# A cross-attention and mixture-of-experts layer: another order in the prologue, and the last token tile in a PSUM bank of its own

## The reference

```python
x = x + attention(_layernorm(x), ctx, ctx, mask)       # q = LN(x) Wq + bq, k = ctx Wk + bk, v = ctx Wv + bv
xf = _layernorm(x).reshape(-1, 256)
scores = sigmoid(_l2norm(xf) @ _l2norm(gate_w).T)      # (4096, 16)
topk_scores, topk_idx = top_k(scores, 8)
combine = one_hot(topk_idx) * topk_scores / sum(topk_scores)
routed = sum_e combine[:, e] * (silu(xf @ w_gate[e]) * (xf @ w_up[e])) @ w_down[e]
shared = silu(xf @ sw_gate) * (xf @ sw_up) @ sw_down
x = x + routed + shared
```

## Time and profile before

| | |
|---|---|
| median of 3 runs | 641.28 us (640.98 to 641.42) |
| profiled execution | 641.74 us, of which span 639.6 us |
| TensorE busy | 99% of the span |
| VectorE, ScalarE, GpSimd busy | 73%, 37%, 43% |
| TensorE in the chain that ended last | 92% |

### The profile page before, as it was taken

One profiled execution on the slowest core, in us unless ns is written; L12 is line 12 of the kernel. 1 busy time (PEld: TensorE's weight loads), 2 busy tenths in 40 slices (PEclk: granted clock), 3 DMA queues, 4 the chain that ended last, 5 costly groups with the idle time before them and its releaser, 6 DMA issues.

```text
span 639.6 us, 10415 instructions
## 1 busy us (share of the span) xinstructions
PE 632.1 (99%) x3690; PEld 550.9 (86%) x3690; DVE 464.7 (73%) x925; ACT 234.6 (37%) x500; POOL 275.4 (43%) x261
## 2 busy tenths in 40 slices
PE   8999999999999999999999999999999999999997
PEld 7688888988889888888888888888888888888886
DVE  3789887759876698767977689766987669575444
ACT  4745544332343324333242333324233332432221
POOL 2527576325533356233653346423562335423342
PEclk9999999999999999999999999999999999999999
DMA  7457562532315324333335232253151431242100
GB/s 206 100 178 218 162 169 44 201 101 73 83 35 182 109 67 99 111 107 119 68 68 188 70 117 66 34 200 108 67 98 38 162 109 46 53 133 101 66 2 33
DMA packets 112512, 67.04 MB, mean 105 GB/s; under 512 B 80981, under 2 KB 102254, under 8 KB 112462
## 3 DMA queue, kind: packets, MB, share of 16 engines
q1 hardware_dynamic: 111374, 65.61, 35.4%
q10 hardware_dynamic: 1088, 0.79, 0.4%
HBM read 55.66 MB, written 10.42 MB: 103 GB/s over the span
## 4 chain that ended last, share of the span: by engine, by line
PE 92%; DVE 3%; DMA 1%; issue 1%; ACT 1%; POOL 1%; SPq 1%; POOLq 0%; ACTq 0%; DVEq 0%
PE gate_ps L399 9%; PE gate_ps L398 9%; PE y_ps L397 9%; PE up_ps L399 9%; PE up_ps L398 9%; PE gate_ps L397 9%; PE y_ps L398 9%; PE up_ps L397 9%; PE y_ps L399 9%; PE f_ps L545 3%; PE up_ps L406 1%; PE f_ps L582 1%; SPq L277 1%; PE f_ps L584 1%; DMA xs<-t_rows 1%
## 5 line engine op out<-in xcount | busy, mean ns | idle before, releaser
L1358 POOL TENSOR_TENSOR hidden<-hidden,cb 128x512 f32<-128x512 f32 x128 | 193.3, 1511 | 288.6 <-DVE hidden L1162 245.6
L880 ACT ACTIVATE hidden<-gate_ps 128x512 f32<-128x512 f32 x136 | 81.3, 598 | 295.0 <-PE gate_ps L399 294.9
L1158 DVE SCALAR_TENSOR_TENSOR hidden<-hidden,gate_ps 128x512 f32<-128x512 f32 x136 | 92.7, 682 | 97.5 <-ACT hidden L880 97.2
L397 PE MATMUL y_ps<-W,hs 128*128 128x256 f32 x544 | 154.2, 283 | 0.6 <-DVE hs L1168 0.6
L398 PE MATMUL y_ps<-W,hs 128*128 128x256 f32 x544 | 151.5, 278 | 0.0
L399 PE MATMUL y_ps<-W,hs 128*128 128x256 f32 x544 | 151.2, 278 | 0.0
L1168 DVE TENSOR_TENSOR hs<-hidden,hs 128x512 fp32r<-128x512 f32 x136 | 105.6, 777 | 22.6 <-ACT hs L887 22.2
L397 PEld LDWEIGHTS y_ps<-W,hs 128*128 128x128 f32 x544 | 102.2, 188 | 7.4 <-issue 1.6
L397 PE MATMUL gate_ps<-xT,W 128*128 128x512 f32 x272 | 107.3, 394 | 0.0
L399 PE MATMUL gate_ps<-xT,W 128*128 128x512 f32 x272 | 107.1, 394 | 0.0
L399 PE MATMUL up_ps<-xT,W 128*128 128x512 f32 x272 | 106.9, 393 | 0.0
(11 more groups left out here) (164 smaller groups left out, 641.1 us busy)
## 6 DMA issues: line engine op xcount, KB each, us to landing
cb<-c_rows SPq DMA_DIRECT2D x64, 512.0 KB, 4.5
blocks<-in_x_dram SPq DMA_DIRECT2D x28, 128.0 KB, 2.9
xin<-in_x_dram SPq DMA_DIRECT2D x7, 512.0 KB, 3.7
t_rows<-blocks SPq DMA_DIRECT2D x28, 128.0 KB, 2.7
xs<-t_rows SPq DMA_DIRECT2D x7, 512.0 KB, 3.6
out_dram<-x SPq DMA_DIRECT2D x7, 512.0 KB, 5.8
p_rows<-blocks SPq DMA_DIRECT2D x28, 80.0 KB, 2.3
stage<-in_L_ffn_w_gate_dram SPq DMA_DIRECT2D x16, 128.0 KB, 2.7
```

What stands on the lines that cost most here:

```text
L397: mm(ps, lh, rh, start=first and i == 0, stop=False)
L880: af(ew[:, i, :], gate_ps[:, i, :], ACT.Tanh, scale=0.5).then_inc(tanh_done, 1)
L1158: V_.scalar_tensor_tensor(out=ew[:, i, :], in0=ew[:, i, :], scalar=1.0, in1=gate_ps[:, i, :], op0=ALU.add, op1=ALU.mult).then_inc(silu_don ...
L1358: pg.tensor_tensor(h[:, i, :], ew[:, i, :], cb[:, pair % PLACES, (e - 1) % 2, :], ALU.mult) \
```

## The change

Three parts. (1) *Prologue.* Wq's load is issued ahead of Wk's and its turns stand first on PE, before ctx; `write_wqT` moves from ACT to DVE, behind `mean_wq` and ahead of `ln1(0, 0)`; the warm-up has 17 turns; SP issues the ctx tails ahead of x and both halves of x ahead of the small vectors; `load_x_blocks(1)` moves ahead of stage 4's load. (2) *Attention ahead.* PE does the scores ahead of the other batches' turns, both turns of the probabilities around `values(0)`, and `attend` ahead of `keys_rest(1)`; `turn_ln2_first` ahead of `keys_by_wq_rest(0)`; `keys_by_wq_rest(1)` behind `turn_z(0)`. ACT's list follows: `split_hi(0)` ahead of the first `exps`, `split_hi(1)` behind `read_keys_rest(1)`. POOL's list is not changed. (3) *Tail.* In the last chunk tile 3 of y is accumulated in `f_ps[:, 0]`; tiles 2 and 3 are added and stored one by one.

```diff
-WARM = 20
+WARM = 17
+        def y_of(c, j):
+            if c == CHUNKS - 1 and j == TILES - 1:
+                return f_ps[:, 0, 0:D]
+            return y_ps[:, j // 2, (j % 2) * D:(j % 2 + 1) * D]
...
             def store_last():
-                for q in range(2):
-                    sp.wait_ge(y_added, upto(CHUNKS - 1, 2, q + 1 + FREE))
-                    sp.dma_start(out_rows[CHUNKS - 1, :, 2 * q:2 * q + 2, :], x2[:, 1, 2 * q:2 * q + 2, :]) \
-                        .then_inc(stored, 16)
+                for i, (j0, j1) in enumerate(((0, 2), (2, 3), (3, 4))):
+                    sp.wait_ge(y_added, upto(CHUNKS - 1, 2, i + 1 + FREE))
+                    sp.dma_start(out_rows[CHUNKS - 1, :, j0:j1, :], x2[:, 1, j0:j1, :]).then_inc(stored, 16)
...
             sp.dma_start(ctx_main[:, 0, :], ctx[0, 0:P, :]).then_inc(ctx0_loaded, 16)
-            sp.dma_start(xin[:, 0:2, :], x_rows[0][:, 0:2, :]).then_inc(x_half, 16)
             sp.wait_ge(tail_zeroed, 1)
             for b in range(B):
                 sp.dma_start(ctx_tail[PAD * b:PAD * b + TAIL, :], ctx[b, P:KEYS, :]).then_inc(ctx0_loaded, 16)
+            sp.dma_start(xin[:, 0:2, :], x_rows[0][:, 0:2, :]).then_inc(x_half, 16)
+            sp.dma_start(xin[:, 2:4, :], x_rows[0][:, 2:4, :]).then_inc(x_loaded, 16)
...
-            sp.dma_start(xin[:, 2:4, :], x_rows[0][:, 2:4, :]).then_inc(x_loaded, 16)
...
             load_stage(STAGES)
+            load_x_blocks(1)
             load_stage(STAGES + 1)
-            load_x_blocks(1)
             move_v_tails()
@@ tensor
             def keys_by_wq_first():
                 pe.wait_ge(wqT_read, 1)
+                pe.wait_ge(kt_read, 2)
...
+                    alone = c == CHUNKS - 1 and j >= 2
-                    ins = three_pass(y_ps[:, j // 2, (j % 2) * D:(j % 2 + 1) * D],
+                    ins = three_pass(y_of(c, j),
...
+                                     first=e == 0 and (j % 2 == 0 or alone),
+                                     last=e == NE - 1 and (j % 2 == 1 or alone))
+                    if e == NE - 1 and (j == 1 or c == CHUNKS - 1 and j == 2):
                         ins.then_inc(y_half, 1)
...
             keep_warm()
+            turn_wq()
             turn_ctx_first()
             turn_x_first(0)
             keys_first()
-            turn_wq()
-            bias_row_first()
             turn_x_first(1)
             keys_by_wq_first()
+            bias_row_first()
+            scores(0, 0)
+            scores(0, 1)
             turn_ctx_rest(0)
             turn_ctx_rest(1)
-            scores(0, 0)
-            scores(0, 1)
             value_tails()
+            turn_p_first(0)
             values(0, y_ps[:, 0, 0:D])
-            turn_p_first(0)
+            turn_p_first(1)
             keys_rest(0)
-            turn_p_first(1)
-            keys_rest(1)
             attend(0, 0)
             attend(0, 1)
+            keys_rest(1)
             values(1, y_ps[:, 0, 0:D])
             turn_router()
             bias_row_rest()
-            keys_by_wq_rest(0)
             turn_ln2_first(0)
             turn_ln2_first(1)
-            keys_by_wq_rest(1)
+            keys_by_wq_rest(0)
             logits(0)
             gate(0, 0)
             turn_z(0)
+            keys_by_wq_rest(1)
             up(0, 0)
@@ scalar
+                act.dma_start(wq_in, Wq.rearrange("(k p) e -> p k e", p=P)).then_inc(wq_loaded, 16)
                 act.dma_start(wk_in, Wk.rearrange("(k p) e -> p k e", p=P)).then_inc(wk_loaded, 16)
-                act.dma_start(wq_in, Wq.rearrange("(k p) e -> p k e", p=P)).then_inc(wq_loaded, 16)
...
             write_keep(0, 2)
-            write_wqT()
+            read_t1_first(1)
+            read_a_first()
+            bias_row_first()
+            write_keep(2, 4)
             read_ctx_tails()
-            bias_row_first()
             router_norms()
-            read_a_first()
-            read_t1_first(1)
-            write_keep(2, 4)
+            split_hi(0)
+            exps(0, 0)
             read_ctx_rest(0)
             read_ctx_rest(1)
-            split_hi(0)
-            split_hi(1)
-            exps(0, 0)
             exps(0, 1)
...
             read_keys_rest(1)
+            split_hi(1)
             split_hi(2)
@@ vector
+            def write_wqT():
+                dve.wait_ge(wq_mean, 1)
+                for m in range(KD):
+                    ins = V_.tensor_scalar(wqT[:, m, :], gate_ps[:, 0, m * D:(m + 1) * D], wq_sum[:, KD + m:KD + m + 1],
+                                           None, ALU.add)
+                ins.then_inc(wqT_read, 1)
...
+            def add_y_last():
+                c = CHUNKS - 1
+                for i, (j0, j1) in enumerate(((0, 2), (2, 3), (3, 4))):
+                    if i < 2:
+                        dve.wait_ge(y_half, CHUNKS + i)
+                    else:
+                        dve.wait_ge(down_done, upto(c, NE, NE + FREE))
+                    v = x2[:, c % 2, j0:j1, :].rearrange("p j d -> p (j d)")
+                    V_.tensor_tensor(v, v, y_ps[:, 0, :] if i == 0 else y_of(c, j0), ALU.add).then_inc(y_added, 1)
...
             dve.sem_inc(y_added, FREE)
+            mean_wq()
+            write_wqT()
             ln1(0, 0)
             spread_bq()
-            mean_wq()
             ln1(0, 1)
```

More of the change, by code:

```diff
@@ L385, in _ @@
             store_last()
-            sp.wait_ge(stored, 16 * (CHUNKS + 1 + FREE))
+            sp.wait_ge(stored, 16 * (CHUNKS + 2 + FREE))
         @block.tensor
@@ L633, in down @@
                     t = slice(j * P, (j + 1) * P)
-                    ins = three_pass(y_ps[:, j // 2, (j % 2) * D:(j % 2 + 1) * D],
+                    alone = c == CHUNKS - 1 and j >= 2
+                    ins = three_pass(y_of(c, j),
                                      [((hs[:, i, HI, t], hs[:, i, LO, t]),
                                        (W[:, e, HI, DN0:DN0 + D], W[:, e, LO, DN0:DN0 + D]))],
-                                     first=e == 0 and j % 2 == 0, last=e == NE - 1 and j % 2 == 1)
-                    if e == NE - 1 and j == 1:
+                                     first=e == 0 and (j % 2 == 0 or alone),
+                                     last=e == NE - 1 and (j % 2 == 1 or alone))
+                    if e == NE - 1 and (j == 1 or c == CHUNKS - 1 and j == 2):
                         ins.then_inc(y_half, 1)
@@ L736, in read_ctx_rest @@
                    ACT.Copy).then_inc(ctxT_read, 1)
[L738 to L744, removed]
             def write_keep(t0, t1):
@@ L1273, in _ @@
                         soon(s + .5, c + 2)
-                add_y(c)
+                if ahead:
+                    add_y(c)
+                else:
+                    add_y_last()
         @block.gpsimd
```

## The result

| | before | after |
|---|---|---|
| median of 6 runs each | 641.41 us (640.98 to 642.33) | **646.41 us** (645.58 to 647.99) |
| ratio after to before | | 1.0078, 95% interval 1.0064 to 1.0092 |
| profiled execution, span | 641.74, 639.6 us | 645.58, 643.7 us |
| scores start | 13.83 | 12.22 |
| logits start | 31.68 | 34.68 |

The change costs 5.0 us by the medians and 3.8 us between the two profiled executions, of which the one of after is its lowest run. 646.0 us was forecast, with 643.7 to 648.5 as the range. All of it arises ahead of the first up projection: from there (its second matmul, since the start of the first lies under the work before it) to the last matmul it is 601.47 us before and 601.20 after.

What follows compares the result with a forecast made beforehand. TensorE, busy 99% of the span, was taken as the bound, so only prologue and tail could matter. Profiled 641.74 plus 4.5 (prologue) and 0.2 (tail) gave 646.4; the median, 0.46 lower, 646.0 us; range 643.7 to 648.5.

Steps and rivals of the forecast that it cites:

- The start and attend: Prologue to attend: scores at 12.3 instead of 13.83, 1.5 us gained; attend at 21.4 after 1.3 us of idle TensorE.
- The queue: GpSimd behind split_hi(1): split_lo(1) ends at 28.35, LayerNorm 2 steps follow, turns at 31.15; SP's stage 4 load at 28.4.
- The last link: Before the logits: stage 4's load lands at 31.9, token copies wait; logits 34.6 instead of 31.68, 2.9 us lost.
- rival (1): TensorE's clock falls to half speed around the idle time before the logits, 2.5 us more: 648.5 us; chance 0.13.
- Rival (4): Before the logits: t2 copies wait only for GpSimd's std chain, not stage 4: 3.3 us slower, 644.5 us; chance 0.10.
- Rival (2): GpSimd's queue behind split_hi(1) doesn't bite, so no change: 642.2 us; chance 0.10.
- Rival (3): The 1.5 us won at the scores reaches the end, with low halves at 20.1 and queue open: 639.8; chance 0.07.
- keys_by_wq_rest(1): TensorE between turn_z and up(0,0): block moved from ahead of the logits, nothing idle to hide it, 1.55 us lost.
- The tail: Behind the last matmul: adds end unchanged, last store issued 0.18 us late, landing 2.1 us: +0.2 us.
- The sum: Up to up(0,0): 2.9 plus 1.55, +4.5 us, start at 38.7; with the tail's +0.2, profiled execution 646.4 us.

Runs made afterwards that it cites:

- Experiment 3: Changed kernel with ACT's split_hi(1) back behind exps(0, 1) and TensorE's keys_rest(1) back ahead of attend: 641.92 us, ratio 0.9992 to before.
- Experiments 1: Changed kernel with one move taken back, ACT's split_hi(1) behind exps(0, 1): 642.49 us, ratio 1.0011 to before.
- experiment 6: Kernel before with one move of the change alone, ACT's split_hi(1) behind read_keys_rest(1): 642.97 us, ratio 1.0016.
- experiment 2: Three runs on the changed kernel: split_hi(4) behind the t2_hi_first copies, 645.65 us; identity turns filling TensorE's idle time, 645.17 us; both, 645.11 us.
- the filled kernel: Changed kernel with 20 identity turns ahead of turn_ln2_first(0) and 4 ahead of turn_ln2_first(1): 645.17 us, ratio 1.0061 to before.
- The first kernel of experiment 4: Changed kernel, split_hi(1) early, keys_rest(1) ahead of attend, keys_by_wq_rest(0) ahead of LayerNorm 2 turns, keys_by_wq_rest(1) ahead of logits, split_hi(4) behind t2 copies: 639.95 us.
- the one with both edits: Changed kernel with the 20 and 4 identity turns and split_hi(4) behind both t2_hi_first copies: 645.11 us, ratio 1.0047 to before.

## Why the prediction was right

**The start and attend.** The scores were put at 12.3 (measured 12.22), attend at 21.4 (21.33) with TensorE idle for 1.3 us before it (1.19). Experiment 3 shows that this idle time has no return.

**The queue.** GpSimd's split was put at 26.45 (26.52), its end at 28.35 (28.33), the second half of the turns at 31.15 (31.28), SP's load at 28.4 (28.41), its landing at 31.9 (31.93). Experiments 1 and 6 show that these are causes and not company.

**The last link** was right in its time and half right in its cause. The low parts were put at 34.45 (34.58) and the logits at 34.6 (34.68), by stage 4's load. But rival (1), the clock, came true as well: granted 0.50 from 30.74 us for 3.41 us. The prediction gave it a chance of 0.13 and charged it with 2.5 us on top. What failed in that rival is the price: the slow matmuls ran inside the wait for stage 4's load, and keys_by_wq_rest(0) grew by 1.0 us, into a wait of 0.93 us that TensorE otherwise has there. The positions in the three runs of experiment 2 show it: without either one alone the logits come 0.3 us earlier at most, without both 1.3 us. The Trainium skill (TensorE: Matmul & The Clock Gate, Part 1: The HAM clock gate) says that idleness throttles the array and activity releases it; the stretches of the changed kernel agree (0.50 behind the 2.35 us of idle time), and so do those of the filled kernel (1.00 from 7.58 us on).

**Rival (4)**, that stage 4 isn't waited for, falls by ACT's row at 31.93. **Rival (2)** falls by GpSimd's 10.21 us. **Rival (3)** named what the faster case needs: the queue open, and TensorE's waits filled. It also asked for the low halves at 20.1 us; that wasn't needed. The first kernel of experiment 4 has the first two alone and took 639.95 us, where that rival said 639.8. But the rival counted on the whole 1.5 us of the scores to reach up(0,0), and 0.94 did: the closeness of the totals is partly chance.

**keys_by_wq_rest(1)** behind turn_z was charged with 1.55 us. From the logits to the second matmul of up(0,0) it was 2.89 us before and 4.26 after: 1.37 us. In the first kernel of experiment 4, where it is back ahead of the logits, that distance is 2.89 again.

**The tail** was charged with +0.2 us and cost nothing: the landing of the last 128 KB was taken at the 2.1 us of 256 KB and took 1.8.

**The sum** up to up(0,0) was +4.5, the whole +4.7. Measured by the second matmul of up(0,0) it was 4.37; the first, put at 38.7, started at 38.35, under the end of keys_by_wq_rest(1). Step by step behind the scores, from the table: the early split gives back 3.40 us (of these, 1.29 also come back in experiment 2 by the load and the clock together; what is left, 2.1, is put down to GpSimd's steps behind the split), keys_rest(1) ahead of attend 0.63, the filled waits 1.33, and 0.62 are left. That makes 5.98, less the 1.61 us won at the scores. Between the two profiled executions 3.84 were measured: 4.37, less 0.27 in the expert loop, 0.05 in the tail and 0.21 outside the span. The medians stand 5.0 apart, since the median of after is 0.8 us above its profiled execution and that of before 0.3 below; single executions scatter by that much. The forecast for the profiled execution (646.4) was 0.8 us too high, so that the median came within 0.4 us of 646.0 is partly chance; the positions are what bears the account out.

## What to carry to other kernels

When a producer is moved back in one engine's list, go through the unchanged lists of the engines that wait for it: here one line on ACT held GpSimd's LayerNorm steps and SP's reload, neither of which needs the block of keys that the line was put behind, and cost 3.4 to 3.9 us. Before work is moved off a chain, ask what TensorE does in the wait that is left; work that filled a wait here cost nothing (keys_rest(1) ahead of attend) and nearly its full length where there was no wait (1.37 of 1.55 us for keys_by_wq_rest(1)). When two chains end within 0.1 us at the same instruction, an experiment that shortens one of them shows next to nothing (0.0 and 0.3 us here, 1.3 for both); take away both.

## What the runs showed that was not expected

- **The clock rises at another time in each execution.** The first record of the full clock stood at 7.07 us before and at 6.84 after; in the other profiled executions, whose first 6 us are nearly the same list, at 5.88, 6.35, 6.72, 6.96, 7.57, 7.58, 7.71 and 7.77. With the same list up to the scores they start at 11.74 us with the rise at 5.88 and at 12.51 with the rise at 7.58. So absolute times in the prologue compare two kernels to no better than 0.8 us, and the table above counts from the scores. In experiment 6, with a wait of 1.56 us in the turns, the record stood at 14.28 and the eight matmuls of keys_first took 2.39 us instead of 1.28. The Trainium skill (TensorE: Matmul & The Clock Gate, What's actually happening) says that the number of slow matmuls at the start varies from run to run of one kernel; these records, of a moment that moves by 1.9 us, agree.
- **A page's clock line is filled in ahead of the first record.** The stretches show 1.00 there, while the warm-up turns stand 0.21 us apart and later ones 0.11. The spacing is the better witness.
- **The clock fell behind a stand of 2.35 us.** In the changed kernel TensorE stood from 27.87 to 30.21 us, did the first turns of LayerNorm 2, and the granted clock was 0.50 from 30.74 us for 3.41 us; with split_hi(4) late it was the same (0.50 from 30.61, for 3.41 us). Stands of 1.19 us ahead of attend, of 1.31 us in the filled kernel and of 1.79 us in the one with both edits, the last two in the expert loop, brought no fall.
- **The kernels with the new start spend 0.35 us less outside the span.** An execution takes longer than its span, from the first to the last instruction. The median of that difference is 1.80 to 1.87 us in each of the eight kernels with the changed start and 2.16 to 2.18 us in the kernel before and the two made from it. What takes this time stays open.
- **The expert loop scatters.** From up(0,0) to the last matmul it took 601.2 to 601.9 us in nine of the profiled executions and 603.0 and 603.6 in the two with identity turns in the prologue, by single waits of 0.3 to 1.8 us in the first chunk. Whether the turns have a part in that stays open.
